# A fused block kernel: attention loop rebuilt, with two unread mask products in each step from the fourth on

## The reference, cut to what matters

```
x = x + xattn0(layernorm(x), ids, ctx)      # 4 gated FFNs of width 256, one picked per token by its id
x = x + ffn0(layernorm(x), Wq..Wd)          # attention with 16 heads of 16, then 8 experts, top 2
x = x + wkv(layernorm(x), ctx)              # a linear recurrence over the tokens
x = x + ffn1(layernorm(x), w1, w2)          # rounded activations, weights rounded to -1, 0, 1

# within ffn0
q, k, v = (rmsnorm(x) @ W.T).reshape(b, s, 16, 16)
attn = softmax(where(causal, q @ k.T * scale, -inf))
x = x + (attn @ v) @ Wo.T
moe: logits = rmsnorm(x) @ Wr.T; top 2 of 8; y = sum p_e * (silu(x Wg_e) * (x Wu_e)) @ Wd_e
```

## Time and profile before

| | us |
|---|---|
| median of three runs | 449.32 |
| the profiled execution | 447.25 |
| its span, first to last instruction | 445.5 |
| TensorE busy (matmul) | 372.1, 84% |
| VectorE busy | 272.0, 61% |
| GpSimd busy | 191.3, 43% |
| ScalarE busy | 154.2, 35% |
| mean granted clock of TensorE | 0.858 of full speed |

### The profile page before, as it was taken

How to read it: one execution, slowest core, us unless ns; L and a number is a source line. 1 busy time by engine, 2 the same in 40 slices (tenths; PEclk the granted TensorE clock), 3 DMA queues, 4 the chain that set the end, 5 groups by cost and what they waited for, 6 DMA issues and landing times.

```text
span 445.5 us, 6878 instructions
## 1 busy us (share of the span) xinstructions
PE 372.1 (84%) x2176; PEld 282.7 (63%) x2179; DVE 272.0 (61%) x799; ACT 154.2 (35%) x337; POOL 191.3 (43%) x253
## 2 busy tenths in 40 slices
PE   6799997798899898876659999995699936875696
PEld 5588876565566564644648888884588824674374
DVE  5786755754535458765623355479743318999983
ACT  3234332133432423540023433331133323332783
POOL 3765243500000000010288799749875117563662
PEclk9899999568958759995559999998899975789899
DMA  7800198984460400000026843043132024000011
GB/s 242 337 2 0 71 143 177 177 121 97 84 84 0 169 1 7 19 25 0 24 82 204 291 167 111 34 143 141 36 107 84 24 85 129 0 1 0 1 37 60
DMA packets 16326, 39.20 MB, mean 88 GB/s; under 512 B 3362, under 2 KB 9956, under 8 KB 14500
## 3 DMA queue, kind: packets, MB, share of 16 engines
q1 hardware_dynamic: 14084, 32.73, 27.3%
q0 software_dynamic: 2208, 6.03, 4.1%
HBM read 29.38 MB, written 9.31 MB: 87 GB/s over the span
## 4 chain that ended last, share of the span: by engine, by line
PE 69%; DVE 18%; issue 4%; ACT 4%; DMA 2%; POOL 1%; POOLq 0%; ACTq 0%; DVEq 0%; SPq 0%
PE bank L1455 11%; PE bank L1456 10%; PE bank L1457 10%; PE bank L1461 7%; PE bank L1516 4%; PE bank L1605 3%; PE bank L1587 3%; DVE junk L1127 3%; PE bank L1673 2%; PE bank L1607 2%; PE bank L1554 2%; PE bank L1627 2%; DVE yc L1109 2%; PE bank L1758 2%; PE bank L1882 2%
## 5 line engine op out<-in xcount | busy, mean ns | idle before, releaser
L641 POOL TENSOR_SCALAR rs_tmp<-rs_tmp 128x2 f32<-128x2 f32 x4 | 1.9, 480 | 124.7 <-DVE rs_tmp L1214 124.7
L1334 DVE TENSOR_TENSOR act_lo<-bank,act_hi 128x512 fp32r<-128x512 f32 x23 | 15.9, 691 | 56.5 <-ACT act_hi L857 56.5
L1127 DVE CUSTOM_DVE_ANT_0 junk<-bank,causal 128x128 bf16<-128x128 f32 (+1 forms) x128 | 37.7, 354 | 20.3 <-PE bank L1587 20.3
L820 ACT ACTIVATE E_sb<-bank 128x384 f32<-128x384 f32 x64 | 27.9, 488 | 38.5 <-PE bank L1609 38.5
L1455 PE MATMUL bank<-we_hi,xg_hi 128*128 x92 | 39.7, 431 | 0.0
L1455 PE MATMUL bank<-we_hi,act_hi 128*128 x92 | 29.2, 318 | 10.3 <-DVE act_lo L1334 10.3
L1456 PE MATMUL bank<-we_lo,xg_hi 128*128 x92 | 37.4, 406 | 0.0
L1457 PE MATMUL bank<-we_hi,xg_lo 128*128 x92 | 37.0, 403 | 0.0
L633 POOL TENSOR_TENSOR we_lo<-we_lo,we_hi 128x3072 fp32r<-128x3072 f32 x5 | 34.6, 6912 | 0.4
L665 POOL DMA_INDIRECT y_dram<-xg,y_row x23 | 22.9, 997 | 22.6 <-ACT xg L862 17.3
L658 POOL DMA_INDIRECT xg<-xn_dram,slot_tok x23 | 22.3, 970 | 13.6 <-DVE slot_tok L1308 7.7
(11 more groups left out here) (268 smaller groups left out, 1014.0 us busy)
## 6 DMA issues: line engine op xcount, KB each, us to landing
we_lo<-in_wexp SPq DMA_DIRECT2D x8, 1536.0 KB, 7.2
qk_dram<-qk_parts SPq DMA_DIRECT2D x8, 512.0 KB, 4.1
q_pack<-qk_dram SPq DMA_DIRECT2D x24, 128.0 KB, 4.5
k_pack<-qk_dram SPq DMA_DIRECT2D x24, 128.0 KB, 7.8
yc<-y_dram SPq DMA_DIRECT2D x8, 256.0 KB, 2.8
...
```

The lines of the kernel that those rows point to most:

```text
L820: a.activation(E_sb[:, n % E_RING, :], bank[4 + n % 2][:, 0:3 * P], ACT.Exp).then_inc(exp_done, 1)
L1127: last = v.tensor_tensor_reduce(out=junk[:, m % 4, t * P:t * P + keys], in0=row_banks(m // 2)[h % 2][:, t * P:t * P + keys], in1=causal[:, ...
```

## The change

The attention loop and what surrounds it are rebuilt:

- Each head's rows in the packs are interleaved: 64 rows, of which every fourth is 0 in q and 1 in k, and the last holds the maximum. The load writes every fourth partition (`slice(64 * odd + c, 64 * odd + 4 * HD, 4)`).
- The maxima are transposed, copied and stored in halves of a sequence (eight groups g, `nm_in[g]`), so only six row pairs stand ahead of the first column pair (FRONT = 6), and two run in each of steps 0 and 1, until the lead is LEAD = 8.
- A column pair waits for each exponential of the pair before on its own.
- The router weights stand beside the value weights, and the joined weights beside `wo`: `v_proj` and `ep_out_logits` now make 264 columns, and `ep_base`, `ep_scale`, and (but for the last sequence) `ep_logits` are gone. `turn_wo` and `join_weights` move into the first stage.
- GpSimd splits experts 0 to 2, in four pieces each. VectorE copies `ho_t`.
- From step 3 on, each step of the loop waits for the last `o_t` copy and then runs `keep_awake(2, bank[6])`, two products of the identity with the mask whose result nobody reads. Eight such products stand in the first stage's last tile.
- `quantise` runs one half per slot in slots 9 to 20, as operations on two tensors: the constant is read from a tile `magic`.

```diff
+        LEAD = 8
+        FRONT = 6
+        NM_AT = {max(2, HH * g - 3): g for g in range(1, 2 * B)}
+        P_AT = {4: 6, 6: 7}
+        W_LOAD_AT, W_ABS_AT, W_MEAN_AT, W_QUANT_AT = 1, 3, 8, 9
+        EP_OT, EP_HT, EP_WO, EP_ADD, EP_RMS = 1, 2, 3, 4, 6
+        V_AT = 6
+        def rows_at(m):
+            first, end = ((min(i + LEAD + 1, FRONT + 2 * (i + 1)) if i >= 0 else FRONT) for i in (max(m, 0) - 1, m))
+            return range(first, min(end, NP))
...
-                            r0 = 64 * odd + HD * c
+                            rows = slice(64 * odd + c, 64 * odd + 4 * HD, 4)
...
+            store_max(5)
             for i in range(TB, 2 * TB):
                 store_x2(i)
+            store_max(6)
+            store_max(7)
...
+            pool.wait_ge(b_xn, NT)
+            split_expert(0, W_PIECES)
             for m in range(NP + HP):
...
+                    if bt + 1 < RING:
+                        split_expert(bt + 1, W_PIECES)
...
+                const = magic[:, pass_no % 2:pass_no % 2 + 1].to_broadcast([P, W_HALF])
+                if pass_no == 0:
+                    last = v.scalar_tensor_tensor(raw, raw, wscale[:, j:j + 1], const, ALU.mult, ALU.add)
+                elif pass_no == 1:
+                    last = v.scalar_tensor_tensor(raw, raw, MAGIC + 1.0, const, ALU.min, ALU.max)
+                else:
+                    last = v.tensor_tensor(dst, raw, const, ALU.subtract)
...
-                if W_QUANT_AT <= s < W_QUANT_AT + 6:
+                if W_QUANT_AT <= s < W_QUANT_AT + 12:
...
+            def keep_awake(n, dst):
                 for _ in range(n):
+                    t_.matmul(dst[:, 0:3 * P], ident_b[:, :], causal_t[:, :], start=True, stop=True)
...
                 for odd in range(2):
+                    if r >= 1:
+                        pe.wait_ge(exp_done, 2 * (r - 1) + odd + 1)
                     t_.matmul(bank[4 + odd][:, 0:3 * P], ident_b[:, :], causal_t[:, :], start=True, stop=False)
...
+            score_row_pair(1)
+            v_proj(0, bank[4:6])
+            for r in range(2, 5):
+                score_row_pair(r)
+            max_rows(0)
             b_product(5)
+            for r in range(5, FRONT):
                 score_row_pair(r)
             b_turn(6)
             for m in range(NP + HP):
                 if m < NP:
                     score_col_pair(m)
+                    if m >= 3:
+                        pe.wait_ge(o_copied, (m - 1) // 2)
+                        keep_awake(2, bank[6])
+                if m == 0:
+                    b_turn(7)
...
                 gidx = quad_at(m)
                 if gidx is not None:
                     weighted_values(gidx)
+                for r in rows_at(m):
+                    score_row_pair(r)
```

446 lines of the change are left out of this document (222 added, 224 removed).

## The result

The changed kernel takes 443.08 us in the median of 20 runs (432.74 to 446.48), the kernel before 448.94 us in as many (443.11 to 459.85); the ratio is 0.973, with a 95% interval of 0.968 to 0.979. That ratio keeps only executions within 1.5% of the fastest of the same kernel, 5 of the 20 of the changed kernel and 14 of the 20 of before; the plain medians are 5.9 us apart, a ratio of 0.987. So the changed kernel is faster, by 6 us (medians) to 12 us (ratio), and not by the 28 that were forecast: the prediction said 420, with a range of 406 to 437. The profiled execution took 444.19 us, with a span of 442.3 us; the one of before that the prediction was built on took 447.25 us, with a span of 445.5.

The account below looks back on a forecast made before the run. TensorE was taken to bound the loop, a fifth of its time there lost to the clock; the expert stage lost 11.6 us around slow rounding. 447.25 - 19.9 (loop end) - 7.8 (experts) = 419.5, said as 420, range 406 to 437.

Parts of the forecast that it names:

- First column pair: End of the ramp: the loop's first column pair starts at 86.5 us, between 84.5 and 88.5, instead of 92.12.
- Steps 0 to 4: Start of the loop: 11.5 us at full clock, 17.0 expected with most at half clock, between 11.5 and 21.7.
- The price of the products: Loop steps: the two unread mask products cost at most 0.35 us in even steps, nothing in odd ones.
- rival D: Odd loop steps: products wait for a late o_t copy, 8 us, 428 in all; part of the main chance 0.62.
- The mean of 0.94: Loop clock: the unread products keep it up once risen; half clock early adds 5.5 us to 82.3.
- The loop end: Attention loop: ends at 177.3 instead of 197.2 us, -19.9, from 86.5 + 82.3 + 5.5 + 3.0.
- Experts: Expert stage: one rounding instruction per slot instead of two saves 7.8 us, between 0.9 and 11.6.
- as a meeting late in a split costs little: Expert stage: reason for putting the remaining blocking of rounding by GpSimd's splits at 3.8 us, of at worst 10.7.
- The worst case per meeting: Expert stage: a rounding instruction meeting a GpSimd split costs 7.04 + 1.23 - 2.9 = 5.4 us; two meetings 10.7.
- the rule that speaks against this edit: Expert rounding: two-SBUF-input VectorE instructions contend with GpSimd's SBUF reads, so the edit only trades one contention for another.
- Case E: Loop: late pack loads or stores of maxima stall column pairs some 5 us per sequence; 441 to 450 us, chance 0.05.
- 82.3 / 115.7: Loop: mean clock of 0.71 at which a slower loop cancels the expert gain, in a rival of chance 0.05.

Follow-up runs that it names:

- b_same: The kernel before, run once more without an edit: 449.81 us beside 449.26 of before, ratio 1.003.
- a_same: The changed kernel, run once more without an edit: 433.39 us beside 436.55 of before, medians only.
- a_same2: The changed kernel, run once more without an edit on another chip: 442.77 us beside 450.16 of before, ratio 0.978.
- a_lateq: The changed kernel with the rounding instructions of before put back, in slots 17 to 22, behind GpSimd's last split: 417.89 us, ratio 0.958 to before.

## Why the prediction was wrong

**First column pair.** 86.5 was said, 87.9 measured (83.5 to 90.6 over the runs with spread packs). Right. What stands behind it was missed: b_turn(7) had been moved to behind the first column pair, and its wait of 3.70 us, for a VectorE instruction held up beside GpSimd's fills of the packs, is in no term of the sum.

**Steps.** Steps 0 to 4 were put at 17.0 us; they took 21.4 (87.94 to 109.29). Without the wait of 3.70 they are 17.7, so the share at half clock was judged well (the bound of 21.7 is not worked out in the prediction; twice 11.5 would be 23.0). From step 5 on 73.8 were forecast and 71.7 measured, both to the first product of the last weighted values. The price of the products was right in the mean: eight steps with an epilogue take 22.2 us with them and 20.9 without, 0.17 per step, where 0.35 in even steps and nothing in odd ones was said. Step by step it is otherwise: from 0.16 less to 0.44 more. The wait for the copy (rival D) did not bind: the profile shows no idle time ahead of line 1553.

**Clock.** The mean of 0.94 was right (0.93 measured) and its reason wrong, which is luck: without the products the clock holds as well, but for one fall of 3.4 us in six profiles. The sentence "With the two products each step fills TensorE with 128-row work" gave them the effect of something else in the rebuild; the removal of ep_base and ep_logits, costed only for the time it frees, is the likeliest.

**The loop end.** -19.9 was forecast and -16.3 is the difference of the two recorded profiles (198.1 and 181.8, where the products end; the forecast's 197.2 and 177.3 are their starts, and 181.0 is what the start came to), but that is against an execution of before in which the clock fell for longer than in any other. Against b_same it is -6.4, of which 3.2 stem from the first column pair. This is the step that failed worst: "177.3 instead of 197.2" took the clock of one profile, 0.80 in the loop, for a property of the kernel, where four others show 0.89 to 0.96 (two of them with an edit there) and a loop end of 185.6 to 189.8. The range of executions shown with the times (448.8 to 459.85) could have warned.

**Experts.** -7.8 was forecast. Like with like it is about nothing: 123.7 us against 122.4, 124.0 and 122.1 without late slots, 136.6 and 130.3 against 133.9 and 131.5 with them. The term that was mis-sized is the blocking that remains, put at 3.8 us "as a meeting late in a split costs little": slots 9 to 15 lose 13.0 us over 5.08 each (13.1 in a_same; 6.5 in a_same2, where slot 9 met no split), as much as before's three lose (11.8). The worst case per meeting was right (7.68 us for one instruction, slot of 9.3), but the instructions now stand in twice as many slots, from one slot earlier, and meet three splits instead of two. The sentence on the rule that speaks against this edit was the better guide: a VectorE instruction with two SBUF inputs contends with a GpSimd instruction that reads SBUF (the Trainium skill, "SBUF — State Buffer", "Who interferes with whom"), and the trace agrees, 7.68 us beside a split of 6.75. And the delay goes further than the slot: the slots are late, so the load of expert 6, which waits for a ring place, is late; GpSimd waits 11.60 us for it at 284.69 (5.94 in a_lateq, with the rounding out of the way), and slot 14 waits for its split (7.3 us, 290.77 to 298.11).

**The sum.** 447.25 - 27.7 was said. Measured as ratio it is -12, by the medians -6, in the pairs of medians of later groups -3 and -7. Of the 16 to 25 us that are missing, some 10 are the baseline's loop, 8 to 9 the rounding, 4 the wait of b_turn(7). The two recorded profiles compared with each other, 447.25 and 444.19 us, look otherwise: the loop end is 3.7 us short of the forecast, and the slots are 22.0 us off, of which 12.8 are the late slots and 9 the rounding. Both accounts hold, since the recorded execution of before had some 10 us too much in its loop and lacked the late slots.

**Rivals.** The range ended at 437, and the median lies 6 us above it. Case E, "little comes of it", had the right size at 0.05, but by stalls of the column pairs for late packs or maxima, which the profile does not show (packs land in 2.7 to 2.8 us in the median, and the wait for maxima is 0.2 us in all). No rival had the baseline in question. Where the prediction says that loop and experts cancel at 82.3 / 115.7, its own terms give 115.5; nothing hangs on it.
